# A fused recommendation tower: six units get layer 0 from products with partners, and the two threads stand 20 slots apart

## The reference, cut to what matters

```python
x0 = xk = embeddings                    # (1024, 32, 16)
for W in (W0, W1, W2):                  # (32, hk, 64), hk = 32 in the first layer and 64 in the others
    xk = relu(einsum('bmd,bhd,mhk->bkd', x0, xk, W))
    outs.append(sum(xk, axis=2))
h = concatenate([concatenate(outs, axis=1), dense_ctx], axis=1)   # 3 * 64 + 16 = 208 columns
h = relu(h @ W_top1 + b_top1); h = relu(h @ W_top2 + b_top2); y = h @ W_top3
```

## Time and profile before

| | |
|---|---|
| median of 3 runs | 623.99 us |
| the profiled execution | 625.95 us, with a span of 624.0 us on the core |
| PE busy | 600.8 us (96%), 2926 matmul passes |
| DVE busy | 515.1 us (83%) |
| POOL busy | 444.2 us (71%) |
| ACT busy | 322.4 us (52%) |
| granted TensorE clock | 0.997 of full speed |

### The profile page before, as it was taken

The page is one execution under the profiler, slowest core; times in us unless marked ns, Lnnn a source line. Parts: engine busy times, 40 slices in busy tenths (PEclk is TensorE's granted clock), DMA queues, the critical chain, the costliest instruction groups (busy, mean ns, idle before and its releaser), DMA issues.

```text
span 624.0 us, 8470 instructions
## 1 busy us (share of the span) xinstructions
PE 600.8 (96%) x2926; PEld 211.4 (34%) x2926; DVE 515.1 (83%) x454; ACT 322.4 (52%) x545; POOL 444.2 (71%) x346
## 2 busy tenths in 40 slices
PE   4779899999999999999999999999999999999998
PEld 3532333333333333333333333333333333333454
DVE  0258698999989998999899998999899999888500
ACT  1333565555565454565545554545565456643564
POOL 6778858788787878787887878786878875556300
PEclk9999999999999999999999999999999999999999
DMA  4597787867887777677767887777667868750000
GB/s 128 184 333 257 283 308 292 285 239 258 274 283 274 258 244 253 222 289 246 258 227 282 283 275 245 252 283 253 222 236 265 289 242 273 269 197 0 1 1 0
DMA packets 45199, 144.49 MB, mean 232 GB/s; under 512 B 9619, under 2 KB 24085, under 8 KB 32870
## 3 DMA queue, kind: packets, MB, share of 16 engines
q1 hardware_dynamic: 36966, 141.85, 62.8%
q0 software_dynamic: 8192, 2.11, 4.0%
HBM read 139.21 MB, written 4.72 MB: 231 GB/s over the span
## 4 chain that ended last, share of the span: by engine, by line
PE 87%; POOL 5%; DMA 5%; issue 2%; SPq 1%; ACT 0%
PE acc L677 77%; POOL gathered L506 5%; PE x_ps L672 5%; DMA x_rows<-gathered 3%; PE sums_ps L746 2%; PE x_ps L746 2%; DMA gathered<-in_table,idx 1%; SPq L419 0%; DMA x_wide<-x_rows 0%; SPq L408 0%; DMA base_sb<-in_base 0%; PE sums_ps L672 0%; POOL idx L529 0%; ACT x_wide L593 0%; ACT x_wide L596 0%
## 5 line engine op out<-in xcount | busy, mean ns | idle before, releaser
L627 DVE TENSOR_TENSOR dve_ring<-x_wide,x_ps 128x1024 f32<-128x1024 f32 x428 | 489.2, 1215 | 62.2 <-issue 47.2
L677 PE MATMUL acc<-dve_ring,w_sb 128*64 128x512 f32 (+1 forms) x1744 | 474.6, 589 | 6.8 <-DVE dve_ring L627 6.8
L506 POOL DMA_INDIRECT gathered<-in_table,idx x256 | 243.8, 952 | 69.7 <-issue 64.1
L518 POOL TENSOR_TENSOR pool_ring<-x_wide,x_sb 128x1024 f32<-128x1024 f32 x84 | 199.3, 2383 | 76.7 <-ACT x_sb L577 46.9
L677 PEld LDWEIGHTS acc<-dve_ring,w_sb 128*64 128x64 f32 x1744 | 150.9, 138 | 293.4 <-issue 268.6
L677 PE MATMUL acc<-pool_ring,w_sb 128*64 128x512 f32 x336 | 131.6, 592 | 0.0
L567 ACT ACTIVATE x_ps<-acc 64x512 f32<-64x512 f32 (+1 forms) x132 | 73.5, 557 | 110.5 <-PE acc L677 108.2
L677 PE MATMUL acc<-pair_squares,w_sb 128*64 128x512 f32 (+1 forms) x264 | 113.9, 581 | 1.2 <-ACT pair_squares L547 1.2
L577 ACT COPY x_sb<-layer_out 64x512 f32<-64x512 f32 x128 | 79.0, 617 | 3.6
L547 ACT ACTIVATE pair_squares<-x_ps 128x1024 f32<-128x1024 f32 x32 | 32.8, 1025 | 88.5 <-PE sums_ps L672 88.2
L572 ACT ACTIVATE layer_out<-acc 64x512 f32<-64x512 f32 (+1 forms) x98 | 56.8, 579 | 2.4 <-PE acc L677 1.0
(11 more groups left out here) (36 smaller groups left out, 127.1 us busy)
## 6 DMA issues: line engine op xcount, KB each, us to landing
x_wide<-x_rows SPq DMA_DIRECT2D x96, 1024.0 KB, 8.0
x_wide<-x_rows SPq DMA_DIRECT2D x32, 768.0 KB, 5.6
x_wide<-x_rows SPq DMA_DIRECT2D x32, 256.0 KB
gathered<-in_table,idx POOLq DMA_INDIRECT x256, 4.5
x_rows<-gathered SPq DMA_DIRECT2D x32, 128.0 KB
w_sb<-in_w SPq DMA_DIRECT2D x2, 512.0 KB, 5.7
x_rows<-gathered SPq DMA_DIRECT2D x32, 16.0 KB
x_wide<-in_W_top SPq DMA_DIRECT2D x1, 512.0 KB, 4.3
```

Source lines behind the costliest of these rows:

```text
L506: pool.indirect_dma_start(gathered[:, c, j % 2, e * DIM:(e + 1) * DIM], None, table, bass.IndirectOffsetOnAxis(ap=idx[:, unit, e:e + 1], a ...
L518: nc.gpsimd.tensor_tensor(pool_ring[:, c], x0_step(c, j, layer, 2 * d, 2).rearrange("p (s n) -> p s n", n=COLS), x_sb[:, layer - 1, c, :]. ...
L627: nc.vector.tensor_tensor(dve_ring[:, c, slot:slot + width, :], x0_step(c, j, layer, i, width).rearrange("p (s n) -> p s n", n=COLS), x_ps ...
L677: done = nc.tensor.matmul(part, w, x[:, cols], start=first, stop=last)
```

## The change

Six units, (0, 4), (0, 6), ... (0, 14), get layer 0 in another way. Their four layer-0 tiles are products instead of squares of sums: SP loads one more tile, the *partners* (256 KB, `load_partners`), ACT copies it into a PSUM bank, and one DVE instruction of 128x2048 (`pairs`) multiplies the first four steps of `x0_wide` with it, broadcast four times. Its weights (`w0p_sb`, a sum of two loaded arrays, and `w0p_diag`) are other ones. PE then has the same five steps, but no burst, and ACT no squares of sums. In thread 1's unit of the same number POOL makes doubles 3 and 7 of layer 2 instead of 5, where it did not before (units 4 to 12).

`DELTA` becomes 20. The burst for (0, 2) moves from slot 4 to slot 10 of (0, 1). At the start the calls of `stage` and `load_first_step` for (1, 0), (0, 1) and (1, 1) stand ahead of loads of blocks that they stood behind.

```diff
+PARTNER, PARTNER_APART = 4, 12
+BY_PRODUCTS = frozenset((0, j) for j in range(4, 16, 2))
-DELTA = 18
+DELTA = 20
@@ sum_slot
-    return begin(c, j) + (4 if j > 0 else (20, 10)[c])
+    if j == 0:
+        return begin(c, 0) + (20, 10)[c]
+    return begin(c, j) + (10 if (c, j) == (0, 1) else 4)
@@ pool_doubles
-    return {1: (6,), 2: ((3, 7), (5,))[c]}[layer]
+    return {1: (6,), 2: ((3, 7), (3, 7) if (0, j) in BY_PRODUCTS else (5,))[c]}[layer]
@@
+def pairs_slot(c, j):
+    return begin(c, j) + 6
@@ pe_order
-            works.append((sum_slot(c, j) + 0.5, "sums", c, j + 1, 0, 0))
+            if (c, j + 1) not in BY_PRODUCTS:
+                works.append((sum_slot(c, j) + 0.5, "sums", c, j + 1, 0, 0))
@@ dve_order
+        if (c, j + 1) in BY_PRODUCTS:
+            works.append((pairs_slot(c, j), "pairs", c, j + 1, 0, 0, 0))
@@ sp_order
             works.append((at + 30, "block", c, j + 2, 0))
+            if (c, j + 2) in BY_PRODUCTS:
+                works.append((at + 32, "partners", c, j + 2, 0))
             works.append((at + 34, "block", c, j + 2, 1))
@@ sync
+            def load_partners(c, j):
+                rows = rows_of(c, j)
+                sp.wait_ge(layer0_done[c], j)
+                sp.dma_start(partner_steps(c),
+                             bass.AP(rows.tensor, rows.offset + PARTNER * COLS,
+                                     [[COLS, FIELDS], [PARTNER_APART * COLS, Q], [1, COLS]])).then_inc(partners_loaded[c], 16)
...
+            sp.dma_start(w0p_sb[:], w0_near).then_inc(pair_weights, 16)
+            sp.dma_start(w0f_sb, w0_far).then_inc(pair_weights, 16)
+            sp.dma_start(w0p_diag[:], w0_diag).then_inc(pair_weights, 16)
...
             load_block(0, 0, 1)
+            load_block(0, 0, 2)
             stage(1, 0)
-            load_block(0, 0, 2)
...
             stage(0, 1)
-            load_block(1, 0, 2)
             sp.wait_ge(x0_staged[0], 64)
             load_first_step(0, 1)
+            load_block(1, 0, 2)
             load_block(1, 0, 3)
-            load_block(0, 1, 0)
-            load_block(0, 1, 1)
             stage(1, 1)
             sp.wait_ge(x0_staged[1], 64)
             load_first_step(1, 1)
+            load_block(0, 1, 0)
+            load_block(0, 1, 1)
@@ scalar: squares
+                if (c, j) in BY_PRODUCTS:
+                    act.wait_ge(partners_loaded[c], 16 * (products_before(c, j) + 1))
+                    act.wait_ge(squares_made, squares_before(c, j))
+                    nc.scalar.copy(sums_ps[:, 0, :], partner_steps(c)).then_inc(partners_placed[c], 1)
+                    act.wait_ge(layer0_done[c], j)
@@ vector
+            def pairs(c, j):
+                wait_first_step(dve, c, j)
+                wait_block(dve, c, j, 0)
+                dve.wait_ge(partners_placed[c], products_before(c, j) + 1)
+                dve.wait_ge(layer0_done[c], j)
+                nc.vector.tensor_tensor(
+                    pair_squares[:, c],
+                    x0_step(c, j, 1, 0, SUM_TILES).rearrange("p (s n) -> p s n", n=COLS),
+                    sums_ps[:, 0, :].unsqueeze(1).broadcast_to([P, SUM_TILES, COLS]),
+                    ALU.mult).then_inc(pairs_made[c], 1)
```

More of the change, by code:

```diff
@@ L133, in dve_groups, with squares_before, sums_before, products_before @@
     return [(i, 2) for i in range(0, STEPS, 2) if not by_pool(c, j, layer, i)]
+def pairs_slot(c, j):
+    return begin(c, j) + 6
+def squares_before(c, j):
+    return sum(1 if (d, n) in BY_PRODUCTS else 3 for n in range(j + 1) for d in range(THREADS) if (n, d) < (j, c))
+def sums_before(c, j):
+    return sum(4 * ((d, n) not in BY_PRODUCTS) for n in range(j + 1) for d in range(THREADS) if (n, d) < (j, c))
+def products_before(c, j):
+    return sum((c, n) in BY_PRODUCTS for n in range(j))
+def squares_of_sums(c, j):
+    return 0 if (c, j) in BY_PRODUCTS else squares_before(c, j) + 1
 def mlp_plan():
@@ L320, in cin_tower @@
         weights_b = sem("weights_b")
+        pair_weights = sem("pair_weights")
         step_weights = sem("step_weights")
@@ L475, in _ @@
                     stage(c, j)
+                elif work == "partners":
+                    load_partners(c, j)
                 elif work == "block":
@@ L543, in squares @@
             def squares(c, j):
[L544 to L549, removed]
+                if (c, j) in BY_PRODUCTS:
[3 more added lines that the diff above has]
+                    act.wait_ge(layer0_done[c], j)
+                else:
+                    act.wait_ge(sums_made, sums_before(c, j) + 4)
+                    bank = sum_banks(c, j)
+                    nc.scalar.activation(pair_squares[:, c, 0:2, :], x_ps[:, bank:bank + 2, :],
+                                         ACT.Square).then_inc(squares_made, 1)
+                    nc.scalar.activation(pair_squares[:, c, 2:4, :], sums_ps[:], ACT.Square).then_inc(squares_made, 1)
                 wait_first_step(act, c, j)
@@ L556, in finish @@
                 wait_layer(act, layer, c, j)
[L558 to L563, removed]
+                if layer == 0 and c == 0 and j > 0 and squares_of_sums(1, j):
+                    act.wait_ge(squares_made, squares_of_sums(1, j))
+                if layer == 0 and c == 1 and 0 < j < UNITS - 1 and squares_of_sums(0, j + 1):
+                    act.wait_ge(squares_made, squares_of_sums(0, j + 1))
+                if layer == 1 and j < UNITS - 1 and (c, j) != (0, 0) and squares_of_sums(c, j + 1):
+                    act.wait_ge(squares_made, squares_of_sums(c, j + 1))
                 if layer < 2:
@@ L649, in _ @@
                     product(c, j, layer, i, width)
+                elif work == "pairs":
+                    pairs(c, j)
                 else:
@@ L655, in sums @@
             def sums(c, j):
-                n = sum_number(c, j)
                 wait_first_step(pe, c, j)
-                if n:
-                    pe.wait_ge(squares_made, 3 * n)
+                if squares_before(c, j):
+                    pe.wait_ge(squares_made, squares_before(c, j))
+                for d in range(THREADS):
+                    if products_before(d, j + (d < c)):
+                        pe.wait_ge(pairs_made[d], products_before(d, j + (d < c)))
                 if c == 0 and j > 1:
@@ L799 @@
         arrays[name] = tiles
+    m, t, q = np.meshgrid(np.arange(FIELDS), np.arange(SUM_TILES), np.arange(Q), indexing="ij")
+    near, far = (m + Q_APART * q + t) % FIELDS, (m + PARTNER + PARTNER_APART * q) % FIELDS
+    twice = ((far - near) % FIELDS == FIELDS // 2) & (near > far)
+    for name, (first, second) in (("w0_near", (near, far)), ("w0_far", (far, near))):
+        tiles = np.where(twice[..., None], np.float32(0), w0[first, second])
+        arrays[name] = tiles.transpose(0, 2, 1, 3).reshape(P, SUM_TILES, HK)
     arrays["of_field"] = np.zeros((P, SUM_TILES, P), np.float32)
```

47 lines of the change are left out of this document (31 added, 16 removed).

## The result

The changed kernel takes 620.11 us, the median of seven runs (619.03 to 621.26); the kernel before takes 624.78 us in seven (623.74 to 627.47). The ratio is 0.993, with a 95% interval of 0.9912 to 0.9948: some 4.4 us faster, where 10.1 were forecast. 613.9 us was wrong, and the range, from 610.8 to 619.5, missed the time by 0.6 us. The profiled execution took 620.34 us with a span of 618.5 us.

The account below looks back on a forecast made before the run. PE's work was taken to set the pace between 77 and 598 us, DVE close behind. 625.95 - 7.3 + 0.8 - 3.6 = 615.85, less 1.96 for the median: 613.9 us, range 610.8 to 619.5.

Parts of the forecast that it names:

- Part 1: PE, steady part: six bursts go at 1.21 us each, restart included, so PE loses 7.3 us.
- The cheap burst: Third rival: on PE each burst removed saves only 0.43 us, six 2.6, giving 618.6 us; chance 0.02.
- Part 1's other estimate: PE's burst by the Trainium skill's ratio 3.07: 0.56 us each, six 3.4 us, time 617.8 us.
- Part 2: DVE's new pairs instruction takes 2.2 us; DVE is late for PE only at (0, 4), costing 0.8 us in all.
- become the bound: First rival: DVE becomes the bound, all its 7.5 us come onto PE, 620.6 us, half 617; chance 0.16.
- Part 3: ACT, POOL, the partner load, extra weight loads and a DVE add at the start: all costed at 0.
- signs of being wrong: PE waiting for DVE every pair, ACT's copies waiting for DMA, late POOL doubles, or bursts saving 0.6 us only.
- the fourth rival: Partner loads come too late for ACT and DVE despite 1.8 us to spare; slower, up to 629 us; chance 0.07.
- Part 4: Start, ahead of 77 us: new order brings first tiles of (1, 1) and (0, 2) in time, gaining 3.6 us.
- Together 3.6 us: Start: 0.96 us at thread 1's first layer-2 step, 0.86 for two thread 0 steps, 1.75 at (0, 2)'s burst.
- A bound that was put aside: Start: block 2 of (0, 0), in front of (1, 0)'s staging and first tile, could lose 1 us; not taken.
- The second rival: The start gives nothing, its units waiting in a chain of DMA, ACT and DVE: 617.5 us; chance 0.11.

Follow-up runs that it names:

- e1: Changed kernel without products, every unit keeping its burst; new start order, later burst of (0, 2) and 20 slots stay: 627.1 us against 624.01 for the kernel before.
- e5: Kernel before with DELTA = 20 and nothing else changed: 626.84 us against 623.61 for the kernel before.
- e4: Changed kernel with one more POOL double in unit (1, 2), layer 2, beside the first pairs: 619.39 us, 0.9931 of the kernel before.
- e2: Changed kernel with the start order, burst slot and 18 slots of the kernel before, so only the six units by products: 621.15 us, ratio 0.9957.
- e13: Changed kernel with block 2 of (0, 0) again behind the staging of (1, 0), no POOL double added: 618.19 us, 0.9897 of the kernel before.
- e9: Kernel before, unchanged, a second profiled execution: 624.38 us.
- e10: Kernel before, unchanged, a third profiled execution: 624.87 us.
- e6: Kernel before with only SP's start order of the changed kernel (18 slots, old burst slot): 628.89 us, ratio 1.0089.
- e7: e4 with block 2 of (0, 0) again behind the staging of (1, 0): 617.22 us, 0.9892 of the kernel before.

## Why the prediction was wrong

**Right: Part 1.** Six bursts were to give 7.3 us. The rear falls from 496.39 us (e1 and e5, 20 slots without products) to 489.28 (e4, with DVE in time): 7.11, or 1.19 a burst. The cheap burst is refuted. Part 1's other estimate, 0.56 us, was worked out wrongly: 0.429 us is the pace of two threads' steps side by side. A matmul alone takes twice that: the two passes of one without a partner, at 578.33 us in the changed kernel, start 0.43 us apart. With 0.86 in place of 0.429 the same division gives 1.12 us (an estimate), near what was measured, so the rows do agree with that ratio. And the four matmuls of a burst do run together, as the starts of their first passes show:

```profile
162.25 0.70 PE L755 MATMUL x_ps<-x_wide,in_pair_sb 32*128 32x512 f32 x2
162.27 0.70 PE L755 MATMUL sums_ps<-x_wide,in_pair_sb 32*128 32x512 f32 x2
...
578.33 1.02 PE L760 MATMUL acc<-dve_ring,w_sb 128*64 128x512 f32 x2
```

**Right: Part 2.** Pairs take 2.28 us, and the next product starts 2.20 behind their start; 2.2 was taken. DVE is late once, at (0, 4), and e4's edit removes 0.86 us; 0.8 was forecast. DVE did not become the bound at 20 slots; at 18 it was late for PE at the pairs (e2), which the prediction did not ask.

**Right: Part 3.** ACT's copies waited 5.5 us for the partners, at most 2.0. The prediction had such waits among its signs of being wrong, with 1.8 us to spare in the fourth rival; the load took that up, but DVE and PE did not wait for it.

**Failed: Part 4, the start.** It was to give 3.6 us and it cost 1.9, the front's 1.6 and the rear's 0.3. Of the 5.5 us between the two, by the ratios, 2.1 are block 2 of (0, 0) put ahead (e13), 1.2 are thread 0's lead that is lost at the end, and 2.2 are gains that did not come: of 0.96 and 1.75 us e13's front has 0.5. The first and the last share are uncertain by a microsecond or more.

"Together 3.6 us" has three pieces. The 0.96 us up to thread 1's first layer-2 step came as 0.73 in the profiled execution, but from one start to another this time moves by more: in three executions of before it is 72.51, 72.28 and 73.31, in two of the changed kernel 71.78 and 73.07. The 1.75 us at the burst of (0, 2) is a wait of one execution; e9 has 0.57 us and e10 none. It cannot be gained whole in a median, and the 1.96 us by which that execution lay above the median, taken off at the end of the sum, had it in part already: 1.0 to 1.4 us of that surplus lie ahead of the burst of (1, 3). Where the wait did go, another came at (1, 2), at (0, 2) or at neither, from one execution to another. The 0.86 us of thread 0's two steps are there all along the run and are lost at its end: by them the rear was to be 0.86 us shorter, and it is 0.31 us longer.

A bound that was put aside weighs as much: "on the other side this block now lies in front of (1, 0)'s staging and first tile, and could lose 1. I take neither." e13 prices it at 2.1 us, 0.9897 against 0.9930, with intervals that overlap by 0.0005. What was missed is that the block meets the gathers, ahead of the staging, and that block 3 waits behind the staging. The Trainium skill ("DMA: Bandwidth & Descriptors", Queues, rings and completion order) says that each DMA engine takes turns between the queues it has work for, a whole packet at a time. A full queue of loads then slows gathers that stand on another queue. This case agrees, with 78 packets of the gathers against 159 from 24 to 27 us, and 28.96 against 27.34 us for the staging.

The sum as measured: -7.11 for the bursts, +0.86 for DVE, +0.31 for the slots, together the rear's -5.94 us; the ratio's -4.4 leaves +1.6 for the front, where -2.7 (0.96 and 1.75) had been forecast. The second rival, that the start gives nothing, was the near one; its 617.5 us missed the end's 1.2 us and the front's loss. The kernel before itself had a median of 624.78 us in its seven runs, 0.8 above the 623.99 that the forecast started from; 0.993 of 623.99 would be 619.6. So most of the 0.6 us beyond the range is this difference, while the gain, 4.4 us of 10.1, was wrong in any case.

**Open.** e1, e5 and e6 lose 3.2, 2.4 and 5.6 us in the front and do not add up, so order, slots and the burst's slot seem to act on each other there; which execution waits at which tile was not settled. e7 and e13 have the lowest ratios, 6.7 and 6.4 us under the kernel before; between these two the runs don't decide.

## What to carry to other kernels

A wait that one profiled execution shows at the start may not be there in the next: before it is counted as a gain, look at it in two or three executions, and don't take off the same surplus twice. A transfer moved ahead in a queue that is already full pushes something else back (here gathers, by 1.6 us), so name what is late next, gathers on other queues included. Split the run where executions begin to agree; behind such a place a change of 0.3 us can be read from single executions, when medians can't tell 1 us.

## What the runs showed of the hardware

The rear came out as 496.07 or 496.08 us in five executions of three kernels, and as 489.26 to 489.30 in four executions of four kernels; between profiled executions of one kernel nearly all of the difference (1.4 us in before, 1.0 in the changed one) arose in the first 128 us, where gathers, stagings and loads are under way together.

The four matmuls of a burst, 32 rows each, start within 0.02 us of each other, and taking such a burst out of a full stream gave 1.19 us.

Where SP's queue took 95 to 97% of the DMA engines' time from 24 to 27 us, the gathers' queue moved 66 to 95 packets; where it took 16 to 51%, the gathers' queue moved 152 to 167.

The granted clock fell behind waits of PE, but not behind each: from 28 to 32 us it was 0.57 in the changed kernel and 0.65 in e13, just behind 2.98 us in which PE waited for DVE; that is a mean over a stretch with both of its levels, 1.2 and 2.4 GHz. Behind the wait of some 2.2 us at the burst of (1, 0) it was 1.00 from 36 to 40 us in the changed kernel (2.19 us) and 0.60 in e4 (2.21 us).
